# Second layer of the convolution's edge network: whole-array matmuls, or 64-row matmuls on the two halves of the array

## What is computed

```
h = silu(edge_scalars @ fc_w1 / sqrt(8)) * 1.679      # [E, 64]
w = h @ fc_w2 / sqrt(64)                              # [E, 256], four columns of 64: w_a w_b w_c w_d
mid0 = w_a * xg0 * ea0
mid1 = w_b * einsum('euc,ec->eu', xg1, ea1) / sqrt(3)
mid2 = (w_c * xg0)[:, :, None] * ea1[:, None, :]
mid3 = (w_d * ea0)[:, :, None] * xg1
agg  = segment_sum(concat(mid0, mid1, mid2, mid3), edge_dst)   # [N, 512]
```

## Time and profile before

| what | value |
|---|---|
| median of three runs | 4983.21 us |
| the three runs | 4983.21, 4990.72, 4969.48 us |
| span of the profiled execution | 4992.4 us |
| PE busy | 3352.9 us (67%) |
| DVE busy | 3087.9 us (62%) |
| ACT busy | 2582.6 us (52%) |
| POOL busy | 2987.0 us (60%) |
| `conv_edges`, first to last addition (L897) | 207.3 to 1672.2 us |

### The profile page before, as it was taken

The page is one execution under the profiler, slowest core; times in us unless marked ns, Lnnn a source line. Parts: engine busy times, 40 slices in busy tenths (PEclk is TensorE's granted clock), DMA queues, the critical chain, the costliest instruction groups (busy, mean ns, idle before and its releaser), DMA issues. The chain is left out here.

```text
span 4992.4 us, 67602 instructions
## 1 busy us (share of the span) xinstructions
PE 3352.9 (67%) x14837; PEld 2067.5 (41%) x14837; DVE 3087.9 (62%) x7986; ACT 2582.6 (52%) x7955; POOL 2987.0 (60%) x3014
## 2 busy tenths in 40 slices
PE   4699999998999872666566656565365556665660
PEld 3344444444444651444344444443244344444440
DVE  7788888888888662455454444566354454554558
ACT  3588888888888421333333333344243333333347
POOL 2365565655656104666676677646576676767756
PEclk8899999999999985677776677777677776777775
DMA  5332222322323223444444444424344444444425
GB/s 163 93 87 85 85 86 85 91 83 85 88 82 86 83 80 114 121 124 116 126 126 115 125 116 125 126 58 140 104 125 114 126 116 124 127 114 125 127 80 158
DMA packets 274595, 541.01 MB, mean 108 GB/s; under 512 B 73156, under 2 KB 161983, under 8 KB 274240
## 3 DMA queue, kind: packets, MB, share of 16 engines
q0 software_dynamic: 134912, 376.36, 27.8%
q1 hardware_dynamic: 132308, 154.29, 9.9%
q10 hardware_dynamic: 7020, 6.40, 0.4%
HBM read 495.47 MB, written 41.31 MB: 108 GB/s over the span
## 5 line engine op out<-in xcount | busy, mean ns | idle before, releaser
L1172 POOL DMA_INDIRECT arena<-h_rows,idx x1856 | 1913.9, 1031 | 1115.0 <-issue 508.3
L1317 PE MATMUL ps<-arena,z 128*128 128x264 f32 x3712 | 1361.6, 513 | 147.5 <-issue 105.0
L768 POOL DMA_INDIRECT arena<-y_rows,idx x928 | 889.3, 958 | 724.6 <-ACT arena L799 344.8
L1236 ACT ACTIVATE z<-z 128x256 f32<-128x256 f32 x928 | 380.3, 410 | 1522.4 <-remote 501.2
L1432 DVE TENSOR_TENSOR z<-ps,z 128x264 f32 x928 | 395.5, 426 | 1184.4 <-remote 427.7
L1317 PEld LDWEIGHTS ps<-arena,z 128*128 128x128 f32 x3712 | 862.2, 251 | 373.3 <-issue 160.7
L797 ACT ACTIVATE arena<-arena 128x128 f32<-128x128 f32 x2784 | 906.2, 391 | 11.4 <-issue 8.9
L842 PE MATMUL ps<-arena 128*128 128x512 f32 x1856 | 894.5, 605 | 8.7 <-issue 5.1
L1288 PE MATMUL ps<-z 128*128 x5568 | 351.6, 176 | 789.0 <-issue 700.4
L1288 PEld LDWEIGHTS ps<-z 128*128 128x128 bf16 x5568 | 299.8, 105 | 990.9 <-issue 937.0
L1228 ACT ACTIVATE z<-iota,dst_x 128x128 f32<-128x128 f32 x1856 | 641.4, 393 | 24.4
(11 more groups left out here) (230 smaller groups left out, 3016.1 us busy)
## 6 DMA issues: line engine op xcount, KB each, us to landing
z<-lo_rows SPq DMA_DIRECT2D x116, 512.0 KB
arena<-h_rows,idx POOLq DMA_INDIRECT x1856
arena<-y_rows,idx POOLq DMA_INDIRECT x928
z<-seg_rows SPq DMA_DIRECT2D x232, 64.0 KB
h_rows<-arena SPq DMA_DIRECT2D x98, 132.0 KB, 1.7
arena<-h_rows SPq DMA_DIRECT2D x98, 132.0 KB, 2.5
res_rows<-z SPq DMA_DIRECT2D x98, 128.0 KB, 1.9
arena<-res_rows SPq DMA_DIRECT2D x98, 128.0 KB, 2.1
```

Source lines behind the costliest of these rows:

```text
L768: pool.indirect_dma_start(out=ring[:, r, :], out_offset=None, in_=s.y_rows, in_offset=bass.IndirectOffsetOnAxis(ap=rows_of[:, u, n:n + 1], ...
L1172: pool.indirect_dma_start(out=ring[:, u * SCORED + n, :], out_offset=None, in_=h_rows, in_offset=bass.IndirectOffsetOnAxis(ap=s.idx[:, u, ...
L1236: nc.scalar.activation(sel[:, q % SELS, :, :].rearrange("p k n -> p (k n)"), away[:, q % 2, :, :].rearrange("p k n -> p (k n)"), ACT.Relu, ...
L1317: last = t.matmul(ps[:, bank[q % 4], 0:ROW], sel[:, q % SELS, k, :], ring[:, u * SCORED + 2 * q + k, :], start=(k == 0), stop=(k == 1))
```

## The change

The second layer of a quad is computed by four matmuls with 64 rows each instead of two with 128: for each pair, one on rows 0 to 63 of the array (first slot) and one on rows 64 to 127 (second slot), 256 columns each. `w2` shrinks to 128x256, `fc_w2` in each half of the rows, and its memset goes. The two slots of a pair now go to different banks (`k` picks the bank), both pairs of a quad share the two banks, and two quads have four banks. `collected` is left with two banks instead of three. PE issues `second` in odd turns only, for a quad, with one signal (`w_ok`) a quad. The waits follow: `second(quad)` waits for `messages(2 * quad - 3)`, `collect(pair)` for `add(pair - 2)`, `silu(quad)` for one count a quad.

```diff
-    w2 = tail[:, RING * FEAT + 4 * P:RING * FEAT + 8 * P]
+    w2 = tail[:, RING * FEAT + 4 * P:RING * FEAT + 6 * P]
     pre = lambda quad: ps[:, quad % 2, 0:256]
-    layer2 = lambda pair: ps[:, 2 + pair % 3, :].rearrange("p (k f) -> p k f", k=2)
-    collected = lambda pair: ps[:, 5 + pair % 3, :]
+    halves = lambda quad: ps[:, 2 + quad % 2 * 2:4 + quad % 2 * 2, :]
+    layer2 = lambda pair: halves(pair // 2)[:, :, pair % 2 * FEAT:(pair % 2 + 1) * FEAT]
+    collected = lambda pair: ps[:, 6 + pair % 2, :]
...
-                sp.dma_start(w2[h * 64:(h + 1) * 64, h * FEAT:(h + 1) * FEAT], a["fc_w2"]).then_inc(wt, 16)
+                sp.dma_start(w2[h * 64:(h + 1) * 64, :], a["fc_w2"]).then_inc(wt, 16)
...
                 if quad >= 2:
-                    act.wait_ge(w_ok, 2 * (quad - 1))
+                    act.wait_ge(w_ok, quad - 1)
...
-            def second(pair):
-                quad = pair // 2
+            def second(quad):
                 pe.wait_ge(h_ok, quad + 1)
-                if pair >= 3:
-                    pe.wait_ge(msg_ok, pair - 2)
-                nc.tensor.matmul(ps[:, 2 + pair % 3, :], h2[:, quad % 2, pair % 2, :], w2, start=True, stop=True).then_inc(w_ok, 1)
+                if quad >= 2:
+                    pe.wait_ge(msg_ok, 2 * quad - 2)
+                for a in range(2):
+                    for k in range(2):
+                        rows = slice(k * 64, (k + 1) * 64)
+                        last = nc.tensor.matmul(halves(quad)[:, k, a * FEAT:(a + 1) * FEAT], h2[rows, quad % 2, a, :], w2[rows, :], start=True, stop=True)
+                last.then_inc(w_ok, 1)
...
-                if pair >= 3:
-                    pe.wait_ge(z_ok, pair - 2)
+                if pair >= 2:
+                    pe.wait_ge(z_ok, pair - 1)
...
-                if pair + 3 < PAIRED:
-                    second(pair + 3)
+                if pair % 2 and pair + 3 < PAIRED:
+                    second((pair + 3) // 2)
                 collect(pair)
...
-            v.memset(w2, 0.0).then_inc(wz, 1)
...
-                dve.wait_ge(w_ok, pair + 1)
+                dve.wait_ge(w_ok, pair // 2 + 1)
```

More of the change, by code:

```diff
@@ L741, in _ @@
         def _(sp):
-            sp.wait_ge(wz, 2)
+            sp.wait_ge(wz, 1)
             for n in range(GROUP):
@@ L847, in _ @@
                 if quad < 2:
-                    second(2 * quad)
-                    if quad < 1:
-                        second(1)
+                    second(quad)
             for pair in range(PAIRED):
```

## The result

Changed kernel: 5102.65 us median of four runs (5102.18 to 5112.27); the kernel before beside it 4986.97. **Ratio 1.0235, interval [1.0212, 1.0259]: slower by 2.3%.** The profiled span went from 4992.4 to 5100.4 us. From the first to the last addition the edge stage took 1581.5 us (205.4 to 1786.8) instead of 1465; the rest, from the first instruction of the next phase on, is 3311 against 3318. So 116 us were added inside the stage and nothing outside it. Lines moved: L834 is now L838 (second layer), L842 L847 (collection), L784 L785 (silu), L883 L885 (first product), L871 L873 (selection), L897 L899 (addition), L756 L757 (SP's load).

What follows compares the result with a forecast made beforehand. PE, ACT and DVE, within 3% of each other, plus pauses bound the edge stage. Terms -14 - 20 + 66 - 0.5 = +31.5 on the span of 4992.4 gave 5024, 9.2 less for the median: 5015 us, range 4885 to 5120.

Steps and rivals of the forecast that it cites:

- lost cover of the collections: Edge stage, rival A and the forecast: collections starting later decide; 5015 us, own range 4975 to 5070, chance 0.40.
- the bank's +66: Collections with two banks: 57 DVE waits before the selection each lose 1.16 us of cover, +66 us, bounds 0 and +148.
- rival C: Second layer on PE: halves run in series, array empties at each mode change, PE is the bound; 5106 us, chance 0.13.
- -20 us for those of the second layer: DVE's waits before L883: earlier second-layer signals save a quarter of 83 us, -20 us, bounds 0 and -83.
- PE's part: Second layer on PE: half-array passes take PE from 2.80 to 2.64 us a pair; the path keeps 0.03, -14 us.
- Five slots and 0.33 of tails: Second layer on PE: eight overlapping passes 1.07 us, mode changes 0.33, against 1.71 removed: -0.31 us a quad.
- my 14: Edge stage: what the path keeps of PE's relief, 464 x 0.03, -14 us.
- 2.77 for ACT: Edge stage: ACT's own need of 2.77 us a pair, which limits what PE's relief can bring.
- my own criterion: DVE's waits: forecast wrong if L871's shrink from 86 us, L883's grow from 83, or time goes outside the edge stage.
- Rival B: PE and second-layer signals: faster if late signals depend on PE being full; 4886 us, or some 4910, chance 0.30.
- Weight loads and pass count: Second layer on PE: eight passes and weight loads for four; loads covered by passes of 0.214 us, costed at nothing.
- the memset: Start of the kernel: a shorter memset of `w2` on DVE, -0.5 us.

Runs made afterwards that it cites:

- r5: The changed kernel again, on the fifth chip beside r6: 5085.62 us, ratio 1.0264 to the kernel before.
- r6: The same kernel as e2 (changed kernel with whole-array second-layer matmuls), on the fifth chip beside r5: 4958.09 us, ratio 1.0012.
- e7: Changed kernel with second-layer matmuls reordered, both pairs on the upper half first, then both on the lower; second chip: 4441.74 us, ratio 0.9914.
- e1: Kernel before with only the collected banks cut from three to two, first chip: 4983.56 us, ratio 1.0062.
- e2: Changed kernel (its banks, order, signals) with the old whole-array second-layer matmuls of 128 rows and 512 columns, first chip: 4958.67 us, ratio 1.0004.
- r4: The same kernel as e2, run on the fourth chip: 5031.88 us, ratio 1.0094.
- d3: Kernel before with bfloat16 second-layer operands, two passes a quad instead of four, fourth chip: 4962.76 us, ratio 0.9956.
- e6: e2 with each 512-column second-layer matmul cut into two of 256 columns, second chip: 4480.2 us, ratio 1.0005.
- r3: The same kernel as e6 (whole-array matmuls cut to 256 columns), run on the third chip: 5138.35 us, ratio 1.0283.
- d1: e6 with four cuts of 128 columns instead of two of 256, sixteen second-layer passes a quad, fourth chip: 5088.75 us, ratio 1.021.
- e8: e2 with three collected banks and the first layer in one bank, issued three quads ahead, second chip: 4476.91 us, ratio 0.9996.
- e5: Changed kernel with each quad's half-array second-layer matmuls issued twice, 16 passes instead of 8, second chip: 4568.67 us, ratio 1.0193.
- r1: The changed kernel again, on the third chip: 5107.89 us, ratio 1.0216.
- r2: The same kernel as e7 (matmuls ordered by halves), run on the third chip: 5107.74 us, ratio 1.0225.
- e4: Kernel before with four collected banks and the first layer in one bank, three quads ahead, first chip: 4950.69 us, ratio 0.9992.

## Why the prediction was right or wrong

- **Direction and range held, the size and the mechanism didn't.** I forecast +0.6% by lost cover of the collections; it was +2.3%. That the sign came out right is luck: it came from the bank's +66, which isn't what was paid. The result lies next to rival C's 5106, and inside a range that C had set, but not by C's mechanism: the halves don't run in series, and PE isn't the bound.
- **The step that failed** is the pricing of PE's late signals: -20 us for those of the second layer, +66 for the collections'. The runs showed the reverse: on DVE the waits for the second layer grew by 109 us (83 to 192, 250 to 1650 us), those for a collection not at all, and the form of the second layer's matmuls, costed at nothing, is worth 137 us (r5 against r6).
- **PE's part: right, undersized.** Five slots and 0.33 of tails for -0.31 us a quad; measured 1.06 for 1.71, -0.65. Where only this counts (e7) it brings 0.9%, 37 us for my 14, until ACT, busy 1193.65 of 1200 us, holds the stage at 2.72; I had 2.77 for ACT. The Trainium skill, "TensorEngine Tiling (Array Packing)", Key Properties, says that changing the tiling mode drains TensorE. The trace leaves at most 0.22 us a quad for both changes, filling included.
- **The third collected bank, +66: too much, and not what was lost.** e1 prices it at 0.6% alone (31 us), and in e2 and r6 the whole rearrangement with two banks costs nothing, in r4, the same kernel, 0.9%. L873's waits, which had to grow beyond 86 us, are 77. That collections wait for additions (173 us) was foretold, but in the pause shown it is a consequence: the addition stands behind L885, which waits for the second layer.
- **The signals of the second layer, -20: wrong in sign, and this is the term that mattered.** By my own criterion (L883's waits growing from 83) I was wrong: 192. I took the lateness of PE's signals as given and asked only how far ahead each was due. Against r6 the waits show that which signal is held up depends on the form of the matmuls; no row of the kernel before could have told that.
- **Rival B's condition, that late signals depend on PE being full: refuted.** PE is less busy and the lateness costs more; d3 gives back 0.4% for half of the second layer's passes.
- **Weight loads and pass count, costed at nothing:** right where signals are on time (e6 1.0005), wrong elsewhere (r3 1.0283; d1 1.0210 beside r4's 1.0094). The cover I named, passes of 0.214 us, was there; the cost isn't in PE's own time.
- **SP: I looked only at whether its loads are as many.** The earlier trace rows shows a late signal, and I wrote that the trace doesn't say what holds it back. SP's queue in the same stretch, seven loads over 13 us where seven take 7 on the second chip, would have shown company for it (timeline before):

```profile
1036.49 13.15 SPq L756 DMA_DIRECT2D arena<-in_ea_rows  x7
```

- The rest held: other phases unchanged, smooth turns of 2.60, and no run shows an effect of the memset or of the loads of `w2`.

**What stays open.** That PE's signals and SP's instructions are slow together, on four chips of five, is seen; which holds up which, or what holds up both, isn't. The record of signals has gaps there too (348 of the collection's 464 in r5, 319 in after; all 464 in e7), and why isn't known either. Nor is what makes the other phases slower there; in one of them, which has none of these loads, ACT stands idle for 1522 us before L1236 in before, for 393 before the same line in e8. A kernel that spreads the eight loads over the pairs, or makes them one, would test it; it wasn't tried. Nor is it known why short passes let the signal of the second layer be held up where long ones mostly don't. The lower clock is more frequent with the change (237 and 301 us of the stage in after and r5, 89 in before, 55 in r6), but r3, whose PE is busy 1039 of 1200 us, has 188 and the largest loss, d1 has some 90 and loses 2.1%, and d3, with some 160, is 0.4% faster. So the clock doesn't order the losses; I take it for a follower of the pauses, which no run shows. e5, meant to keep the array busy, ran on the chip without pauses and can't answer it. No version beats both kernels where signals are late, but for d3's 0.4% in another number format; where they are on time, the halves (e7) beat the kernel before by 0.9%. The change in its own order wasn't run there; r1 and r2 make no difference between the orders.

## What to carry to other kernels

When three engines are within 3% of each other and the stage has pauses, as here, what a change does to the time of one can matter less than which signal is due during a pause: look for the period of the pauses in the loops (here eight pairs, SP's loads) before pricing any cover. Price a form of an instruction by swapping that form alone with the same buffers and order, side by side on one chip, and look at a second chip before calling it a loss or a gain: here the same kernel (e7, r2) is 0.9% faster on one and 2.2% slower on another.

## What was not expected of the hardware

- The same kernel takes 4479 us on one chip and 4946 to 4997 on four. In the edge stage (1289.5 us in e8, 1462 to 1497 in e1, e2, e4 and r6, whose ratios are within 1% of it) signals of PE arrive late on the four, 8 us in the pause of r5, where nearly all of DVE's pauses lie beside a group of SP's loads; the larger part of the difference, in the other phases, isn't explained.
- Matmuls of 64 rows on the two halves ran wholly side by side: 0.85 us for eight passes of 256 columns (e5 against e7), and 1.07 us from first pass to collection in either order of issue.
- Eight whole-array passes of 256 columns in place of four of 512 cost nothing on the chip without late signals (1.0005 against e8's 0.9996), and on one with them the same kernel is 2.8% slower than before, with PE busy 1039 of 1200 us.
